# A two-layer graph attention block: layer-1 mask by DMA transpose and GpSimd, layer-2 feature copy on VectorE, new orders of work

## The reference, cut to what matters

```python
h = jnp.maximum(_layernorm(x), 0.0)
# gat_layer(x, mask, W, a_src, a_dst, bias), run twice, elu between the two:
xl = (x @ W).reshape(B, N, H, F)
asrc = jnp.einsum('bnhf,hf->bnh', xl, a_src)
adst = jnp.einsum('bnhf,hf->bnh', xl, a_dst)
e = jax.nn.leaky_relu(asrc[:, :, None, :] + adst[:, None, :, :], 0.2)
e = jnp.where(mask[..., None], e, -1e9)          # mask = (adj > 0) | eye
attn = jax.nn.softmax(e, axis=1)
out = jnp.einsum('bsdh,bshf->bdhf', attn, xl) + bias
# then
x = x + gat(h)
h = jnp.maximum(_layernorm(x), 0.0)
x = x + h + einsum(h, weights summed over both directions) + label bias of adj
```

## Time and profile before

| | us |
|---|---|
| median of 3 runs (498.0 to 501.19) | 498.49 |
| the profiled execution, its own time | 501.3 |
| its span, first to last instruction | 499.5 |

### The profile page before, as it was taken

One profiled execution on the slowest core, in us unless ns is written; L12 is line 12 of the kernel. 1 busy time (PEld: TensorE's weight loads), 2 busy tenths in 40 slices (PEclk: granted clock), 3 DMA queues, 4 the chain that ended last, 5 costly groups with the idle time before them and its releaser, 6 DMA issues. The chain is left out here.

```text
span 499.5 us, 15008 instructions
## 1 busy us (share of the span) xinstructions
PE 471.8 (94%) x3428; PEld 424.6 (85%) x3428; DVE 428.5 (86%) x1885; ACT 399.6 (80%) x1476; POOL 320.2 (64%) x492
## 2 busy tenths in 40 slices
PE   4488999999999999999999999999999999999875
PEld 1367899999999999999999999999999999999853
DVE  7977888888888988898888988898888988888654
ACT  3247988889888988888888988888888888888831
POOL 2435767676666667766766667766766676766631
PEclk9989999999999999999999999999999999999996
DMA  8011111111111111111111111110111111000001
GB/s 233 21 33 34 36 49 39 56 55 43 36 54 54 54 33 53 54 54 30 46 54 54 54 33 53 54 54 27 48 54 54 54 33 53 22 23 25 21 23 42
DMA packets 29146, 23.70 MB, mean 47 GB/s; under 512 B 1976, under 2 KB 28860, under 8 KB 29120
## 3 DMA queue, kind: packets, MB, share of 16 engines
q1 hardware_dynamic: 27328, 21.44, 14.0%
q10 hardware_dynamic: 1792, 1.98, 1.4%
HBM read 14.56 MB, written 8.39 MB: 46 GB/s over the span
## 5 line engine op out<-in xcount | busy, mean ns | idle before, releaser
L444 ACT ACTIVATE L<-L,nmax 128x128 f32<-128x128 f32 x256 | 99.1, 391 | 5.4 <-DVE nmax L746 3.9
L331 POOL TENSOR_TENSOR h_lo<-h,h_hi 128x512 fp32r<-128x512 f32 x64 | 82.0, 1282 | 24.4 <-DVE h2n L704 20.2
L347 POOL TENSOR_TENSOR P<-L,rsum 128x512 f32<-128x512 f32 x64 | 66.6, 1041 | 20.0 <-DVE rsum L752 18.6
L932 PE MATMUL pY<-w_hi,h_hi 128*128 128x258 f32 x256 | 76.3, 298 | 1.4 <-POOL h_lo L331 1.4
L933 PE MATMUL pY<-w_lo,h_hi 128*128 128x258 f32 x256 | 72.7, 284 | 0.0
L934 PE MATMUL pY<-w_hi,h_lo 128*128 128x258 f32 x256 | 72.3, 282 | 0.0
L460 ACT ACTIVATE elu_e<-pA,minus_ones 128x512 f32<-128x512 f32 x64 | 44.0, 688 | 32.0 <-PE pA L920 32.0
L920 PE MATMUL pA<-PT,xl 128*128 128x128 f32 x512 | 67.7, 276 | 0.5 <-ACT PT L452 0.5
L758 DVE SCALAR_TENSOR_TENSOR h<-elu_e,pA 128x512 f32<-128x512 f32 x64 | 44.0, 688 | 22.8 <-ACT elu_e L460 20.0
L920 PEld LDWEIGHTS pA<-PT,xl 128*128 128x128 f32 x512 | 62.2, 192 | 0.7 <-ACT PT L452 0.7
L746 DVE CUSTOM_DVE_ANT_0 L<-pZ,L 128x128 f32<-128x128 f32 x256 | 58.7, 286 | 3.0 <-ACT L L439 2.9
(11 more groups left out here) (154 smaller groups left out, 1584.2 us busy)
## 6 DMA issues: line engine op xcount, KB each, us to landing
x_all<-in_x SPq DMA_DIRECT2D x32, 256.0 KB, 2.8
out<-x_all SPq DMA_DIRECT2D x32, 256.0 KB, 2.2
adj_all<-in_adj SPq DMA_DIRECT2D x32, 128.0 KB, 2.6
x_all<-in_L_gnn_W ACTq DMA_DIRECT2D x2, 512.0 KB, 6.3
rhs<-lhs SPq DMA_DIRECT2D x64, 6.0 KB
rhs<-lhs SPq DMA_DIRECT2D x64, 1.0 KB
x_all<-in_L_gnn_weights ACTq DMA_DIRECT2D x2, 256.0 KB, 7.3
x_all<-in_L_gnn_att_src ACTq DMA_DIRECT2D x1, 128.0 KB, 6.3
```

Source lines behind the costliest of these rows:

```text
L331: pool.tensor_tensor(h1_lo[p][:, :, :].rearrange("p a b -> p (a b)"), h1[p][:, :], h1_hi[p][:, :, :].rearrange("p a b -> p (a b)").bitcast ...
L347: pool.tensor_tensor(P1[p][:, :, :], L1[p][:, :, :], rsum1[p][:, :].unsqueeze(2).broadcast_to([128, H, 128]), ALU.mult).then_inc(s_P1, 1)
L444: last = act.activation(L1[p][:, h, :], L1[p][:, h, :], ACT.Exp, bias=nmax1[p][:, h:h + 1], scale=-1.0, accum_out=sum1[p][:, h:h + 1])
L932: pe.matmul(pY[:, 0:C2], h1_hi[p][:, k, :], w2_hi[:, k, :], start=(k == 0), stop=False)
```

## The change

- `scores1` no longer has the mask product (L902). Instead SP's new step `transpose_mask` turns each graph's 128 x 128 bf16 mask by a transposing DMA, SBUF to SBUF, into `mask_by_dst` (two DMAs in every second slot), and POOL's new step `mask1` adds it to the four heads of `L1` after `extra1`; `leaky1` waits for `mask1`.
- `features2` moves from ACT to DVE and adds b2 to `pY` as it copies; `add_bias2` on POOL is dropped and `residual1` reads x as it is.
- The four `weigh` steps use one fused multiply-and-sum instruction per block (8 per vector of layer 1, 128 columns each; 4 per vector of layer 2, 256 columns each) in place of product and reduction. The second and later loads of the start wait until W1 has landed.
- All five lists get new orders and lags.

```diff
+        def turned(g, p):
+            return 4 * (g - p) + 16
...
             def load(g, p):
...
+                elif g:
+                    sp.wait_ge(s_w1dma, 16)
...
+            def transpose_mask(g, p):
+                if p % 2:
+                    return
+                if after(g, 4):
+                    sp.wait_ge(s_M1, g - 2)
+                else:
+                    sp.wait_ge(s_mask, g + 2)
+                for j in range(2):
+                    sp.dma_start(mask_by_dst[:, p + j, :], of_graph(mask_all, g + j, N), transpose=True).then_inc(s_turned[p + j], 16)
...
-            pipeline(sp, [(store, 7), (spread_src2, 3), (spread_src1, -1), (load, -6)])
+            pipeline(sp, [(spread_src1, 0), (spread_src2, 3), (transpose_mask, -2), (store, 6), (load, -6)])
...
             def inverse_std1(g, p):
...
-                if after(g, 4):
-                    pool.wait_ge(s_hn, g - 2)
...
+            def mask1(g, p):
+                pool.wait_ge(s_turned[p], turned(g, p))
+                pool.wait_ge(s_sc1, g + 1)
+                pool.tensor_tensor(L1[p][:, :, :], L1[p][:, :, :], mask_by_dst[:, p, :].unsqueeze(1).broadcast_to([128, H, N]),
+                                   ALU.add).then_inc(s_M1, 1)
...
-            def add_bias2(g, p):
-                if first(g):
-                    pool.wait_ge(s_less, 1)
-                pool.wait_ge(s_hn, g + 1)
-                pool.tensor_tensor(of_graph(x_all, g, D), of_graph(x_all, g, D), b2_bc[:, :], ALU.add).then_inc(s_xb, 1)
...
-            pipeline(pool, [(inverse_std1, -3), (low_w1, -2), (mask_off_diagonal, -2), (add_bias2, 1), (low_w2, -1), (inverse_std2, 4), (normalise1, 0), (normalise2, 3), (pause_norm2, 4), (split_h1, 1), (pause_norm1, -3)])
+            pipeline(pool, [(inverse_std2, 5), (low_w1, 0), (pause_norm2, 5), (normalise1, 1), (low_w2, -1), (normalise2, 4), (mask1, 0), (split_h1, 2), (pause_norm1, -2), (mask_off_diagonal, -4), (inverse_std1, -3)])
...
-            def features2(g, p):
-                act.wait_ge(s_ab2, g + 1)
-                if after(g, 2):
-                    act.wait_ge(s_attn2, g - 1)
-                act.activation(xl2[p][:, :], pY[:, 0:D], ACT.Copy).then_inc(s_xl2sb, 1)
...
-            pipeline(act, [(high_w1, -4), (copy_b1, -4), (exp1, 1), (relu_h, -1), (elu_exp, 2), (score_rows2, 3), (exp2, 4), (no_edges, -4), (score_rows1, -1), (high_w2, -2), (high_h1, 2), (extra1, 0), (copy_PT2, 4), (features2, 3), (copy_PT1, 1), (place_label_rows, 4), (relu_h2, 5), (extra2, 3)])
+            pipeline(act, [(high_w1, 0), (relu_h, -1), (score_rows2, 3), (extra1, 0), (high_h1, 2), (high_w2, -1), (copy_PT2, 4), (score_rows1, -1), (copy_PT1, 1), (copy_b1, -3), (no_edges, -5), (relu_h2, 5), (exp1, 0), (extra2, 3), (place_label_rows, 4), (elu_exp, 1), (exp2, 3)])
...
+            def weigh(rows, vector, products, sums, width):
+                blocks = vector.shape[1] // width
+                for k in range(rows.shape[1]):
+                    for b in range(blocks):
+                        cols, m = slice(b * width, (b + 1) * width), k * blocks + b
+                        last = dve.tensor_tensor_reduce(products[:, m * width:(m + 1) * width], rows[:, k, cols], vector[:, cols],
+                                                        1.0, 0.0, ALU.mult, ALU.add, sums[:, m:m + 1])
+                return last
...
             def leaky1(g, p):
-                dve.wait_ge(s_sc1, g + 1)
+                dve.wait_ge(s_M1, g + 1)
...
+            def features2(g, p):
+                if first(g):
+                    dve.wait_ge(s_less, 1)
+                dve.wait_ge(s_xl2, g + 1)
+                if after(g, 2):
+                    dve.wait_ge(s_attn2, g - 1)
+                dve.tensor_tensor(xl2[p][:, :], pY[:, 0:D], b2_bc[:, :], ALU.add).then_inc(s_xl2sb, 1)
...
             def residual1(g, p):
                 dve.wait_ge(s_attn2, g + 1)
-                dve.wait_ge(s_xb, g + 1)
+                dve.wait_ge(s_hn, g + 1)
...
-            pipeline(dve, [(features1, 1), (sum_w3, 0), (recip1, 1), (low_h, -1), (largest_labels, 6), (largest_of_rows, 6), (weigh_w2_dst, 0), (count1, 0), (count2, 3), (elu_max, 2), (recip2, 4), (stats1, -4), (weigh_w2_src, -1), (weigh_w1_src, -2), (layer_norm2, 5), (release1, -4), (low_rows1, -1), (aggregate1, -4), (residual2, 6), (leaky1, 0), (release2, 4), (layer_norm1, -2), (residual1, 4), (label_terms, 3), (take_off_excess, 1), (split_w3, 0), (low_h2, 5), (stats2, 4), (leaky2, 3), (aggregate2, 4), (high_scores2, 2), (weigh_w1_dst, -2), (zero_counts, 2), (low_scores2, 2), (largest_label, 9)])
+            pipeline(dve, [(zero_counts, 2), (stats1, -4), (release1, -4), (count1, 0), (count2, 3), (residual2, 6), (take_off_excess, 2), (weigh_w1_src, -2), (largest_labels, 5), (largest_of_rows, 5), (aggregate1, -4), (low_rows1, -1), (leaky1, 0), (weigh_w2_src, 0), (residual1, 4), (label_terms, 3), (release2, 4), (layer_norm1, -2), (weigh_w2_dst, 0), (stats2, 4), (sum_w3, 1), (low_h2, 5), (aggregate2, 4), (features1, 0), (split_w3, 3), (recip1, 0), (leaky2, 3), (high_scores2, 2), (layer_norm2, 4), (low_scores2, 2), (elu_max, 1), (recip2, 3), (weigh_w1_dst, -2), (low_h, -2), (features2, 2), (largest_label, 8)])
...
             def scores1(g, p):
-                pe.wait_ge(s_mask, g + 1)
                 if after(g, 1):
                     pe.wait_ge(s_max1, g)
-                pe.matmul(pZ[:, :].rearrange("p (h s) -> p h s", h=H), of_graph(mask_all, g, N),
-                          ident_bf[:, :].unsqueeze(1).broadcast_to([128, H, 128]), start=True, stop=False)
                 pe.wait_ge(s_src1[p % 2], copied(g, p))
                 pe.matmul(pZ[:, :], lhs1[p][:, :], rhs1[p][:, :, :].rearrange("p h s -> p (h s)"),
-                          start=False, stop=True).then_inc(s_z1, 1)
+                          start=True, stop=True).then_inc(s_z1, 1)
...
-            pipeline(pe, [(spread_b1, -1), (transpose_P1, 2), (transpose_h2, 6), (attend2, 5), (sum_w2, 1), (scores2, 4), (project2, 3), (transpose_h, -1), (transpose_w3, 0), (attend1, 2), (transpose_scores2, 3), (scores1, 0), (convolve, 6), (score_terms1, -1), (project1, 0), (transpose_P2, 4), (gather_top_label, 8)])
+            pipeline(pe, [(transpose_scores2, 3), (project1, 0), (transpose_P2, 4), (score_terms1, -1), (transpose_P1, 1), (transpose_w3, 2), (attend2, 4), (transpose_h2, 5), (attend1, 1), (scores2, 3), (spread_b1, -2), (sum_w2, 1), (project2, 2), (transpose_h, -2), (convolve, 5), (scores1, -1), (gather_top_label, 7)])
```

More of the change, by code:

```diff
@@ L105, in gat_graphconv_block @@
         mask_all = sb("mask_all", [128, G * N], BF16)
+        mask_by_dst = sb("mask_by_dst", [128, TURN, N], BF16)
         n0_all = sb("n0_all", [128, G])
@@ L231, in gat_graphconv_block @@
         s_bn1, s_mv1, s_rs1a, s_rs1, s_hn = (sem(n) for n in ("bn1_done", "mv1_done", "rs1a", "rs1", "hn_done"))
-        s_n0, s_mask, s_xb = sem("n0_done"), sem("mask_done"), sem("x_biased")
+        s_n0, s_mask, s_M1 = sem("n0_done"), sem("mask_done"), sem("masked1")
+        s_turned = [sem(f"mask_turned{p}") for p in range(TURN)]
         s_T0, s_hThi, s_hTlo = sem("T0"), sem("hThi"), sem("hTlo")
@@ L564, in weigh_w1_src @@
                 dve.wait_ge(s_spread, 1)
-                link(dve.tensor_tensor(w1_att[:, 0, :].rearrange("p (k n) -> p k n", k=KD), w1_f[:, :, :],
-                                       pA[:, :].unsqueeze(1).broadcast_to([128, KD, HF]), ALU.mult))
-                dve.tensor_reduce(w1_scores[:, 0, :], w1_att[:, 0, :].rearrange("p (m f) -> p m f", f=FH), AX.X, ALU.add)
+                weigh(w1_f, pA[:, :], w1_att[:, 0, :], w1_scores[:, 0, :], FH)
             def weigh_w1_dst(g, p):
@@ L572, in weigh_w1_dst @@
                 dve.wait_ge(s_spread, 2)
-                link(dve.tensor_tensor(w1_att[:, 1, :].rearrange("p (k n) -> p k n", k=KD), w1_f[:, :, :],
-                                       pZ[:, :].unsqueeze(1).broadcast_to([128, KD, HF]), ALU.mult))
-                link(dve.tensor_reduce(w1_scores[:, 1, :], w1_att[:, 1, :].rearrange("p (m f) -> p m f", f=FH), AX.X, ALU.add))
+                link(weigh(w1_f, pZ[:, :], w1_att[:, 1, :], w1_scores[:, 1, :], FH))
                 cols = w1_scores[:, :, :].rearrange("p j (k h) -> p k j h", k=KD)
@@ L589, in weigh_w2_src @@
                 dve.wait_ge(s_w2dma, 64)
-                link(dve.tensor_tensor(w2_att[:, 0, :].rearrange("p (k n) -> p k n", k=KH), w2_f[:, :, :],
-                                       att2_bc[:, 0, :].unsqueeze(1).broadcast_to([128, KH, D]), ALU.mult))
-                dve.tensor_reduce(w2_scores[:, 0, :], w2_att[:, 0, :].rearrange("p (k n) -> p k n", k=KH), AX.X, ALU.add)
+                weigh(w2_f, att2_bc[:, 0, :], w2_att[:, 0, :], w2_scores[:, 0, :], D)
             def weigh_w2_dst(g, p):
@@ L596, in weigh_w2_dst @@
                     return
-                link(dve.tensor_tensor(w2_att[:, 1, :].rearrange("p (k n) -> p k n", k=KH), w2_f[:, :, :],
```

(4 more changed lines are left out.)

## The result

The changed kernel takes 538.23 us (median; 536.18 to 539.0) against 498.49 before: a ratio of 1.076, 95% interval 1.073 to 1.079. It is slower by 40 us, and lies outside the forecast range of 485 to 513. The profiled execution took 539.0 us, its span is 537.0 us, 37.5 more than before.

The account below looks back on a forecast made before the run. The prediction took PE to bound a steady slot of 7.03 us, unchanged by the edit. Start +1, 63 slots x 0 and end -3 gave -2 us: 496.5 us from 498.5, range 485 to 513, the forecast's own 492 to 502.

Parts of the forecast that it names:

- x = 0.94: SP's queue: each transposing DMA takes 0.94 us including its gap, hidden with 0.6 us to spare.
- PE's own work, -0.23: Steady slot on PE: dropping L902 saves 0.23 us, so PE's work falls from 7.03 to 6.80 us.
- The stall before attend1, +0.19: Steady slot on PE: the copy of P1's transpose takes 1.28 us, covered by 1.09, so PE stands 0.19 us.
- The extra change of product, +0.04: Steady slot on PE: one more change between full-precision and reduced-precision products costs 0.04 us, between zero and 0.23.
- 6.97 to 7.2: Bounds in us for the steady slot's period, forecast at 7.03, if the stall ahead of attend1 stands.
- 4.28 + 2x: Time in us from transpose_scores2 until scores1's rows are in place, x per transposing DMA; hidden up to x = 1.26.
- rival SP late: SP's transposing DMAs take 1.5 us each, delaying scores1 0.5 us in 31 slots: +16 us, 512.5 us; chance 0.22.
- DVE, POOL, ACT: Steady slot: DVE rises to 6.66 to 6.74 us, POOL to about 5.3, mask1 takes 1.2; no cost, ACT has room.
- Start, +1: Start phase: fused-step savings against the load's wait for W1, mask1 and features1's place; +1 us, between -3 and +4.
- -4 us of the fused steps: Start phase on DVE: the fused weigh steps of layers 1 and 2 take 4 us less DVE time.
- Wrong outright if the start moves by more than 5 us: The prediction's own refutation sign: a start phase moved by more than 5 us makes it wrong outright.
- End, -3: After the last scores1: attend1 follows 8.8 us behind instead of 11.8, same chain behind it; -3 us, between -5 and 0.

Follow-up runs that it names:

- start_order: w1_early with weigh_w2 steps at the head of DVE's list and sum_w2, transpose_w3, take_off_excess, label_terms, sum_w3, split_w3 at earlier lags: 498.38 us.
- one_per_slot: The changed kernel with SP issuing one transposing DMA in every slot instead of two in every second one: 517.85 us.
- scores2_first: The changed kernel with one transposing DMA a slot, no wait of the second load for W1, and scores2 ahead of attend1 on PE: 504.23 us.
- w1_early: scores2_first with the split of W1 earlier, high_w1 at lag -2 on ACT and low_w1 at lag -1 on POOL instead of 0: 505.46 us.
- before_no_mask: The kernel before the change without the mask product L902 and nothing in its place, so its output is not the reference's: 490.54 us.
- pair_with_store: The changed kernel with the pair of transposing DMAs at lag -1 instead of -2 on SP, in the slots with the store: 525.42 us.
- load_early: The changed kernel without the wait of the second load for W1, nothing else: 533.47 us.
- wait_w1: start_order with the second load's wait for W1 put back: 502.36 us.
- before_fused: The kernel before the change with only the four weigh steps fused: 497.63 us, ratio 0.996.
- attend_late_one: one_per_slot with attend1 moved behind project2 in PE's order: 530.09 us.
- w1_late: start_order with the split of W1 back at lag 0 on ACT and POOL: 497.84 us.

## Why the prediction was wrong

Two steps of the prediction failed: SP's time for a transposing DMA (x = 0.94, hidden; it is 1.47 and cost 20.4 us in all), and the start (+1 us; it is +14.4, of which 2.6 are SP's too). A third, that attend1's products take longer behind a wait, was left out of the sum. The profiled executions of after and start_order lie 41.6 us apart: 15.5 us up to the seventh scores1, 25.8 in the 57 slots behind it, 0.2 after that. In the slots the pair is 0.310 us a graph (after and one_per_slot) and the stall ahead of attend1 0.146 (one_per_slot and scores2_first), together 0.456 of the 0.453 lost. In the medians, 39.8 us apart, the pair is 20.4 us, the wait for W1 4.8, the single steps of the start 7.1, less 1.2 that w1_early cost. That leaves 8.7 us for the stall; it is a remainder and not a run of its own, but its slots alone give 57 x 0.146 = 8.3. start_order stands level with the kernel before.

- **PE's own work, -0.23.** In the old order it was too much: 0.167 measured. What is left of the pair is not half of it. Timeline of before_no_mask, PE:

```profile
267.57 0.30 PE L940 MATMUL pC<-ident_r,ab 128*72 128x128 f32 x1
267.71 0.45 PE L903 MATMUL pZ<-rhs,lhs 128*128 128x512 f32 x1
268.00 0.28 PE L974 MATMUL pF<-w_hi,h2T_hi 128*128 128x256 f32 x1
```

  The step of scores1 takes 0.29 us for 0.46, the 0.17 us of the slot. In the new order, where transpose_scores2 follows scores1, it does take the 0.23 us forecast (256.20 to 256.43 in pair_with_store).
- **The stall before attend1, +0.19.** Right in mechanism, nearly right in size: 1.32 us of chain against 1.09 of cover, 0.23. What was missed is what follows a wait. The earlier trace rows showed attend1 at 1.16 us behind a wait and the earlier trace rows at 1.06 without one, in the kernel before. After a wait the eight products take 1.00 us, without one 0.89 in scores2_first and 0.82 in the kernel before: 0.11 to 0.18 us more in every slot, never priced.

```profile
272.98 1.06 PE L920 MATMUL pA<-PT,xl 128*128 128x128 f32 x8
273.80 0.30 PE L942 MATMUL pC<-ident_r,ab 128*72 128x128 f32 x1
```

- **The extra change of product, +0.04.** Not seen as a term of its own. 7.034 - 0.167 + 0.23 + 0.18 = 7.277, and one_per_slot has 7.131: the new list has 0.15 us less elsewhere. The timelines show most of it at scores1 and transpose_scores2: the two steps take 0.46 + 0.14 = 0.60 us before, 0.43 in before_no_mask, and 0.29 in the kernel after (242.60 to 242.89), where they follow each other, 0.14 less. Without the pair the slot came out at 7.13 us, inside the 6.97 to 7.2 given.
- **SP, x = 0.94: the step that failed first.** The place stood, the terms did not. x is 1.47: the nearest row, the issue of a copy, was not near, since 1.12 to 1.20 us of SP go to one transposing issue and not 0.74. The last term of 4.28 + 2x was off too: 1.7 us was read from the copy of 1 KB for layer 2, spread_src2, while scores1 needs one of 6 KB, spread_src1. In the kernel after, where scores1 waits in a steady slot, it starts 2.05 to 2.38 us behind the issue of its copy. In the long slot shown the count from transpose_scores2 (242.83) is 0.64 + 0.78 + 2.93 + 1.05 + 2.16 = 7.56 us, where 4.28 and x = 1.47 give 7.22; PE gets to scores1 after 6.9 us when nothing is late. So the limit was nearer to 1.1 than to 1.26, and x = 0.94 would still have been hidden: x decides. The rival SP late, with x = 1.5 and +16 us, is what happened: the pair costs 0.310 us a graph, 17.7 us over 57 graphs, and 2.6 in the start. It priced a pair at 0.5 us; by the table it is 0.62, and in the slot shown scores1 is 7.56 - 6.91 = 0.65 late, since the copy takes longer than counted. The chance of 0.22 leaned on a row of another operation. The Trainium skill (VectorE: DVE Perf Modes, "The three transpose paths") gives 1309 ns for a 128 x 128 bf16 transpose by DMA. The trace has 1.2 us of issue and about 2.2 us to landing, so the page's figure lies near the time that SP is held, and the issue row of a copy, 0.74, does not.
- **DVE, POOL, ACT.** DVE does not bound: 90.2% of 7.13 us in one_per_slot is 6.43 us, less than the 6.66 to 6.74 taken. mask1 is 1.17 us for 1.2 and hidden. These steps stood.
- **Start, +1: came +14.4, the other step that failed.** The wait for W1 moved the second load's issue from 1.82 to 6.76 us and stats1 of graph 2 from 8.46 to 14.41, by 6.0 us and not by the 2 taken; without the wait the seventh scores1 starts 7.7 us sooner (load_early; 6.0 in the better order, wait_w1). SP's pair is 2.6 us there, the place of the single steps 6.4 (start_order). Against these stand 3.3 us of the fused steps (before_fused). The four were read in different orders and need not add up. The prediction named weigh_w2 and sum_w2, but set their delays against each other instead of following one graph through the chain hn, hT, scores' rows, DMA, scores1. The -4 us of the fused steps were a fair size, 2.4 to 3.4 measured. "Wrong outright if the start moves by more than 5 us" held.
- **End, -3.** attend1 of the last graph comes 9.5 us behind its scores1 and not 11.8, 2.3 sooner and not 3. But "the chain behind it is the same" was not true: it takes 26.1 us for 23.9, in the new order, and the gain is gone. Which step of it is longer is open.

The forecast's slower side held one mishap at a time. Here SP's lateness, attend1's longer products and the start fell together, and none hid another.

## What to carry over

An operation that no row shows holds its queue for a time of its own. Until it is measured, the limit from which it decides (1.26 us in the forecast, about 1.1 in fact) carries more of the verdict than the nearest row of another operation, and each term of that limit has to be read from the very transfer that it stands for. Issue such operations one a slot rather than two in every second: the sum is the same and the fullest slot decides. Where a product has to wait, add what it takes longer behind the wait; and a copy between two products wants just enough cover, since work moved further back starts a chain that has an end to meet. The start is a chain too: after a new order, each single step of preparation has to be placed again, in the idle time that the trace shows.

## What was not expected of the hardware

- SP needs 1.12 us to issue one 128 x 128 bf16 transposing DMA within SBUF and 2.40 for two, against 0.63 to 0.79 for the small copies and 0.38 to 0.41 for a load or a store of 128 partitions. Its median time from issue to landing is 2.2 us.
- A small copy within SBUF was in use 1.64 us after its issue (1 KB, spread_src2), one of 6 KB (spread_src1) 2.05 to 2.38 us after it, where scores1 waited for it in the steady slots of the kernel after.
- attend1's eight products take 1.00 us behind a wait for their data, 0.82 to 0.89 us without one. The first weight load begins with the first product in the kernel after (1.00 us), 0.03 to 0.06 us ahead of it in scores2_first (0.89), and 0.10 to 0.12 ahead both in the kernel before (0.82) and in attend_late_one (0.89). So a weight load that is no longer covered fits the 1.00; it does not explain 0.89 beside 0.82, and no run separates the two.
- In the start of the kernel after, products of 512 columns follow each other every 0.43 us until 39 us, every 0.23 us from 48 us on, while the granted clock reads 1.00 in both stretches. PE was busy 9.0 us between 20 and 39 us, with several waits, and 8.3 us between 39 and 48. The granted clock in these rows does not explain the change of pace, and no run shows what does.
- Fused weigh steps do not escape GpSimd. In w1_late two of them run long while POOL subtracts W1's high part:

```profile
19.17 2.22 DVE L573 CUSTOM_DVE_ANT_0 x_all<-x_all 128x256 f32<-128x256 f32 x1
...
21.32 1.37 DVE L573 CUSTOM_DVE_ANT_0 x_all<-x_all 128x256 f32<-128x256 f32 x1
...
22.62 0.41 DVE L573 CUSTOM_DVE_ANT_0 x_all<-x_all 128x256 f32<-128x256 f32 x1
```

  POOL's instruction runs from 18.77 for 2.35 us there, and mask1 from 21.07 for 1.34. The rule of the Trainium skill (SBUF — State Buffer, "Who interferes with whom") that a DVE instruction with two SBUF inputs and a GpSimd one that reads SBUF shut each other out agrees with this trace: 2.22 and 1.37 us for 0.41.
